# Attention scores of two units at once: float32 products of 64 contraction rows in place of split bf16 products of 128

## What is computed

```python
# x: (8, 224, 2048), context: (8, 750, 512), 32 query heads of 64, 8 key/value heads, 4 query heads to each
q = layernorm(x)                                     # split into 8 groups x 4 heads x 64
k = v = context                                      # split into 8 heads x 64
scores = einsum('bsgrd,btgd->bgrst', q, k) / 8 + mask     # mask: (224, 750)
out = einsum('bgrst,btgd->bsgrd', softmax(scores), v)
x = x + tanh(g_xattn) * out
# then layernorm(x), a routed memory of 512 slots, a small gelu network and a gate, added to x
```

## Time and profile before

| What | Value |
|---|---|
| median of 3 runs | 1175.29 us (1174.78 to 1175.48) |
| the profiled execution | 1174.98 us, its span 1173.1 us, granted clock 0.999 |
| TensorE busy | 1150.5 us (98% of the span) |
| VectorE busy | 947.2 us (81%) |
| ScalarE busy | 912.7 us (78%) |
| GpSimd busy | 889.6 us (76%) |
| chain that ended last | TensorE 76%, GpSimd 20% (its line L593 14%, L560 2%) |
| L593 (GpSimd), 448 times | 1469 ns each |
| L1312 (VectorE), 448 times | 938 ns each |
| L726 and L722 (ScalarE), 448 times each | 917 and 809 ns |
| L912, 896 times, and L923, 896 times | records of 384 and 267 ns |

### The profile page before, as it was taken

The page is one execution under the profiler, slowest core; times in us unless marked ns, Lnnn a source line. Parts: engine busy times, 40 slices in busy tenths (PEclk is TensorE's granted clock), DMA queues, the critical chain, the costliest instruction groups (busy, mean ns, idle before and its releaser), DMA issues.

```text
span 1173.1 us, 35389 instructions
## 1 busy us (share of the span) xinstructions
PE 1150.5 (98%) x14656; PEld 907.2 (77%) x14656; DVE 947.2 (81%) x2269; ACT 912.7 (78%) x1226; POOL 889.6 (76%) x804
## 2 busy tenths in 40 slices
PE   5999999999999999999999999999999999999997
PEld 3888888888888888888888888888887655655553
DVE  5888888888888888888888888888874899676775
ACT  5899898888898888898899988898881444655544
POOL 6899999999999999999999999999992110314222
PEclk9999999999999999999999999999999999999999
DMA  9421231133114212411331131122126500012224
GB/s 337 150 69 48 57 117 42 55 75 106 41 43 107 80 49 53 121 42 55 69 111 42 42 73 52 48 53 57 43 79 187 234 2 1 1 59 87 108 99 153
DMA packets 60735, 95.09 MB, mean 81 GB/s; under 512 B 35233, under 2 KB 44449, under 8 KB 56482
## 3 DMA queue, kind: packets, MB, share of 16 engines
q1 hardware_dynamic: 59858, 91.79, 25.7%
q10 hardware_dynamic: 720, 1.05, 0.3%
HBM read 71.75 MB, written 20.97 MB: 79 GB/s over the span
## 4 chain that ended last, share of the span: by engine, by line
PE 76%; POOL 20%; DMA 1%; DVE 1%; issue 1%; ACT 1%; DVEq 0%; SPq 0%; POOLq 0%
POOL arena L593 14%; PE psum L988 13%; PE psum L912 12%; PE psum L935 12%; PE psum L942 6%; PE psum L923 6%; PE psum L965 5%; PE psum L959 5%; PE psum L960 5%; PE psum L1069 3%; POOL arena L560 2%; PE psum L975 2%; PE psum L890 2%; POOL arena L613 1%; PE psum L1038 1%; POOL arena L601 1%
## 5 line engine op out<-in xcount | busy, mean ns | idle before, releaser
L593 POOL TENSOR_TENSOR arena<-arena 128x768 bf16<-128x768 f32 x448 | 651.6, 1469 | 39.7 <-ACT arena L722 37.1
L1312 DVE CUSTOM_DVE_ANT_0 arena<-psum,arena 128x750 f32<-128x750 f32 x448 | 420.3, 938 | 127.1 <-PE psum L923 121.4
L722 ACT ACTIVATE arena<-psum 128x768 f32<-128x768 f32 x448 | 362.3, 809 | 89.4 <-PE psum L942 89.3
L726 ACT ACTIVATE arena<-arena,neg_max 128x750 f32<-128x750 f32 x448 | 410.9, 917 | 3.8 <-DVE neg_max L1312 3.7
L912 PE MATMUL psum<-arena 128*128 128x512 bf16 x896 | 272.1, 384 | 0.8 <-DVE arena L1209 0.8
L935 PE MATMUL psum<-ident,arena 128*128 128x128 f32 x1792 | 268.4, 272 | 0.0
L959 PEld LDWEIGHTS psum<-arena 128*128 128x128 bf16 (+1 forms) x2688 | 194.7, 98 | 57.5
L960 PE MATMUL psum<-arena 128*128 128x64 bf16 (+1 forms) x2688 | 222.0, 193 | 0.0
L959 PE MATMUL psum<-arena 128*128 128x65 bf16 (+1 forms) x2688 | 221.7, 194 | 0.0
L960 PEld LDWEIGHTS psum<-arena 128*128 128x128 bf16 (+1 forms) x2688 | 178.5, 98 | 53.2
L935 PEld LDWEIGHTS psum<-ident,arena 128*128 128x128 f32 x1792 | 206.3, 140 | 4.3
(11 more groups left out here) (166 smaller groups left out, 1301.3 us busy)
## 6 DMA issues: line engine op xcount, KB each, us to landing
arena<-in_k_t SPq DMA_DIRECT2D x128, 187.5 KB, 3.2
arena<-in_v_rows SPq DMA_DIRECT2D x64, 192.0 KB, 2.5
out<-arena SPq DMA_DIRECT2D x12, 1024.0 KB, 3.9
arena<-in_x_top SPq DMA_DIRECT2D x8, 1024.0 KB, 5.4
arena<-in_x_rest SPq DMA_DIRECT2D x8, 768.0 KB, 4.6
spill<-arena SPq DMA_DIRECT2D x96, 64.0 KB, 2.2
arena<-spill SPq DMA_DIRECT2D x6, 1024.0 KB, 10.6
arena<-in_w_t SPq DMA_DIRECT2D x4, 1024.0 KB, 20.4
```

What stands on the lines that cost most here:

```text
L593: pool.tensor_tensor(p_lo[:, n % RING, :], p_sb[:, n % RING, :], high(p_sb[:, n % RING, :]), ALU.subtract).then_inc(p_split, 1)
L722: act.activation(p_sb[:, n % RING, :], flat_ps[:, turned_at(n):turned_at(n) + CW], ACT.Copy).then_inc(evac_a, 1)
L726: act.activation(s_sb[:, n % RING, 0:CTX], s_sb[:, n % RING, 0:CTX], ACT.Exp, bias=neg_max[:, n % 4, :], scale=-1.0).then_inc(exped, 1)
L1312: dve.tensor_tensor_reduce(s_sb[:, n % RING, 0:CTX], flat_ps[:, score_at(n):score_at(n) + CTX], mask_sb[:, max(n % UNITS - REP + 1, 0), :] ...
```

## The change

Scores of two units, a and a + 1 with a even, are computed together by `score_pair`, as float32 products straight from `q_t` and `k_raw`. `q_t` is now float32 and holds both halves of a transposed block as they come: an even unit has its 64 contraction rows in partitions 0 to 63, an odd one in 64 to 127. So each product uses one half of the array's rows. The columns of the two units are cut in three steps, so that the two halves never write one bank in the same step; a semaphore (`middle_written`) orders the two writers of the middle bank. `score_pair(k + 4)` stands at the start of every even step, ahead of the transposes, and waits until the maxima of both units of the pair before are done (`maxed >= a`).

As halves alternate with the unit's number and a window has seven units, query heads 0 and 1, and 2 and 3, change places in odd windows (`m ^ g % 2` in `add_part`), and one block of the further rows is normalised with its two heads swapped, in two instructions (`crossed`).

`split_k`, `k_lo`, `split_q` and `round_q` are gone. VectorE makes one full-height float32 copy of the query blocks per window; ScalarE makes the three first ones (`copy_first`). VectorE's maximum waits for both units of a pair, and the odd one also for the transposes of the unit three before, whose buffer it overwrites. `DVE_EVACS` is empty, so all copies of transposed exponentials stay on ScalarE.

```diff
+        SCORE_STEPS = ((slice(512, 750), slice(238, 476)), (slice(0, 274), slice(476, 750)), (slice(274, 512), slice(0, 238)))
...
-            def split_k(g):
-                pool.wait_ge(k_loaded[g % 2], 32 * (g // 2 + 1))
...
-                pool.tensor_tensor(k_lo[:, g % 2, :], k_raw[:, g % 2, :], high(k_raw[:, g % 2, :]),
-                                   ALU.subtract).then_inc(k_split, 1)
...
+                if j == 1:
+                    dst, src = crossed(xn_rest[:, j, :]), crossed(xb[:, b % 3, j, :])
+                    act.activation(dst[:, :, 1, :], src[:, :, 0, :], ACT.Identity, bias=bias, scale=scale)
+                    act.activation(dst[:, :, 0, :], src[:, :, 1, :], ACT.Identity, bias=bias, scale=scale).then_inc(rest_normed, 1)
...
+            def copy_first(i):
+                turns = FIRST_TURNS[i]
+                act.wait_ge(q_turned, i + 1)
+                act.activation(q_t[:, 0, turns[0]:turns[-1] + 1, :],
+                               mix_ps[:, FIRST_BANK[i], 0:128 * len(turns)].rearrange("p (t n) -> p t n", n=128), ACT.Copy).then_inc(q_first, 1)
...
-                    kk = high(k_raw[:, g % 2, cols]) if i == 0 else k_lo[:, g % 2, cols]
-                    pe.matmul(flat_ps[:, score_at(n) + cols.start:score_at(n) + cols.stop], q_t[:, pair % 2, half, turn, :], kk,
-                              start=(i == 0), stop=(i == 1))
...
+            def score_pair(a):
+
+                pair, at = divmod(a, 2 * UNITS)
+                for n in (a, a + 1):
+                    g = n // UNITS
+                    if n % UNITS == 0:
+                        pe.wait_ge(k_loaded[g % 2], 32 * (g // 2 + 1))
+                if pair == 0 and at in (0, REP, REP + 2):
+                    pe.wait_ge(q_first, {0: 1, REP: 2, REP + 2: 3}[at])
+                if pair >= 1 and at in (0, REP + 2):
+                    pe.wait_ge(q_copied, 2 * pair - 1 if at == 0 else 2 * pair)
+                if a >= 2:
+                    pe.wait_ge(maxed, a)
+                for i, step in enumerate(SCORE_STEPS):
+                    for half in range(2):
+                        n = a + half
+                        rows, cols = slice(D * half, D * half + D), step[half]
+                        if i == 2 and half == 1:
+                            pe.wait_ge(middle_written, a // 2 + 1)
+                        mm = pe.matmul(flat_ps[:, score_at(n) + cols.start:score_at(n) + cols.stop], q_t[rows, pair % 2, turned_slot(n), :],
+                                       k_raw[rows, n // UNITS % 2, cols], start=True, stop=True)
+                        if i == 0 and half == 0:
+                            mm.then_inc(middle_written, 1)
+                        if i == 2:
+                            mm.then_inc(scored, 1)
...
+                if k % 2 == 0 and 0 <= k + 4 < NU:
+                    score_pair(k + 4)
                 if 0 <= k + 2 < NU:
                     turn_main(k + 2)
                     turn_mid(k + 2)
-                if 0 <= k + 5 < NU:
-                    score_main(k + 5)
                 if k >= 0:
                     value(k)
...
-                if 0 <= k + 5 < NU:
-                    score_mid(k + 5)
...
-                        xs = xa[:, b, slot * GW + m * D:slot * GW + m * D + D]
+                        at = slot * GW + (m ^ g % 2) * D
+                        xs = xa[:, b, at:at + D]
...
-                    dve.wait_ge(scored, n + 1)
+                    dve.wait_ge(scored, n // 2 * 2 + 2)
+                    if n % 2 == 1 and n >= RING:
+                        dve.wait_ge(turned, n - RING + 1)
...
-                    for half in range(2):
-                        dve.tensor_copy(q_t[D * half:D * half + D, pair % 2, half, turns[0]:turns[-1] + 1, :],
...
-                if m in (4, 5) and 1 <= pair < PAIRS:
-                    split_q((window + 1) % 2, pair, m - 4, turn_range(window), 2 * (window + 3) + m - 4 + 1)
...
+                    dve.tensor_copy(q_t[:, pair % 2, turns[0]:turns[-1] + 1, :],
+                                    mix_ps[:, (window + 1) % 2, 0:128 * len(turns)].rearrange("p (t n) -> p t n", n=128)).then_inc(q_copied, 1)
```

More of the change, by code:

```diff
@@ L50 @@
 RING = 3
+DVE_EVACS = ()
 def high(ap):
@@ L61, in evac_on_dve @@
 def evac_on_dve(n):
-    return False
+    return n % (2 * UNITS) in DVE_EVACS
 def evacs_before(n, on_dve):
-    whole, part = divmod(n, UNITS)
-    return sum(whole + (1 if m < part else 0) for m in range(UNITS) if evac_on_dve(m) == on_dve)
+    whole, part = divmod(n, 2 * UNITS)
+    return sum(whole + (1 if m < part else 0) for m in range(2 * UNITS) if evac_on_dve(m) == on_dve)
 def flamingo_block(nc, x_top, x_rest, k_t, v_rows, mask, g_x, av_t, wvd_t, w1_t, wq_t, wr, wr_rows_in, keys_t, log_rel, rel, b1, w2, wvu_t,
@@ L915, in score_mid @@
-            def score_mid(n):
-                g = n // UNITS
-                half, turn = turned_slot(n)
-                if n >= 1:
-                    pe.wait_ge(maxed, n)
-                for i in range(2):
-                    cols = score_cols(n, False)
-                    kk = high(k_raw[:, g % 2, cols]) if i == 0 else k_lo[:, g % 2, cols]
-                    mm = pe.matmul(flat_ps[:, score_at(n) + cols.start:score_at(n) + cols.stop], q_t[:, g // 2 % 2, half, turn, :], kk,
-                                   start=(i == 0), stop=(i == 1))
-                mm.then_inc(scored, 1)
+            def score_pair(a):
[22 more added lines that the diff above has]
+                            mm.then_inc(scored, 1)
@@ L951, in value @@
                         pe.wait_ge(x_added, g - 1)
-                    pe.wait_ge(q_split, min(2 * g + 6, 4 * PAIRS + 2) if g else 4)
+                    if g == 0:
+                        pe.wait_ge(q_first, 2)
+                    else:
+                        pe.wait_ge(q_copied, min(g, GROUPS - 2))
                 evac_wait(pe, n)
@@ L1202, in merge_rest @@
                 ins.then_inc(rest_merged, 1)
-            def split_q(bank, pair, half, turns, count):
-                if pair == 0:
-                    dve.wait_ge(q_hi_done, count)
-                else:
-                    dve.wait_ge(q_hi_own, count - 6)
-                dve.tensor_tensor(q_t[D - D * half:2 * D - D * half, pair % 2, half, turns[0]:turns[-1] + 1, :],
-                                  mix_ps[D * half:D * half + D, bank, 0:128 * len(turns)].rearrange("p (t n) -> p t n", n=128),
-                                  q_t[D * half:D * half + D, pair % 2, half, turns[0]:turns[-1] + 1, :],
-                                  ALU.subtract).then_inc(q_split, 1)
-            def split_first(i):
-                for half in range(2):
-                    split_q(FIRST_BANK[i], 0, half, FIRST_TURNS[i], 2 * i + half + 1)
             for c in range(4):
```

84 lines of the change are left out of this document (24 added, 60 removed).

## The result

The changed kernel takes **1289.76 us** (median of 4 runs, 1289.23 to 1290.19) against 1175.08: 1.0975 times the kernel before, 95% interval 1.0956 to 1.0995, so 114.7 us more. The forecast was 1336, in a range of 1230 to 1570.

What follows compares the result with a forecast made beforehand. TensorE was taken to bound the attention, 448 units times its pitch. Scores with switches 114, copy wait 29, maxima 21, less 3 for removed work, made +161 us on the profiled execution: 1336 us, range 1230 to 1570.

Steps and rivals of the forecast that it cites:

- Passes of the scores: Score products on TensorE: halves overlap, but twelve float32 passes take seven steps in program order, 1.49 us a pair.
- Switches: TensorE going into row halves and out to float32 transposes once a pair: 0.32 us, bounds 0 and 0.5.
- Wait for the copy: Second unit's last two transposes wait for ScalarE's copy of the first: 0.13 us a pair, +29 us.
- Wait for both maxima: Next pair's scores wait for VectorE's second maximum; stalls of 0.41 (even windows) and 0.24 us (odd), +21 us.
- Taken away at nothing: GpSimd's key split and VectorE's query copies and differences, removed, were hidden by TensorE; only -3 us shows.
- A: Rival: score products of the two halves run one after the other, no overlap; about 1562 us; chance 0.20 including partial overlap.
- B: Rival: cheap switches, full overlap of the score products, no wait for the copy; about 1247 us; chance 0.15.
- C: Rival: faster, a pair of scores with its switches below 1.30 us; 1161 us; chance 0.05.
- The estimate of near 1.6 us: Score pair at a like share of 2x, after the skill's 3.07x for four row tiles; between 1.49 and A.

Runs made afterwards that it cites:

- full_height_float32: Changed kernel with the score products of both units taken over all 128 partitions, so no switch into halves; 1518.97 us, ratio 1.2925.
- both pairs of runs: Changed kernel, scores in one half against full height: 1571.91 and 1518.97 us; changed kernel plus one 4-column product, 64 against 128 rows: 1369.16 and 1315.87 us.
- additions_after: Changed kernel with all seven additions of a window behind the second maximum of a pair, not split around the first; 1274.94 us, ratio 1.0848.
- no_key_split: Kernel before with the low part of the keys made for the first two windows alone; 1174.44 us against 1175.16, ratio 0.9991.
- one_half_only: Changed kernel with the score products of both units taken from partitions 0 to 63, so none run side by side; 1571.91 us, ratio 1.3376.
- both_orders: Changed kernel with value products ahead of transposes in odd steps and all additions behind the second maximum; 1259.45 us, ratio 1.0715.

## Why the prediction was right, point by point

The direction and the three places of the loss (scores with their switches, the copy, the second maximum) were right; the sum was 161 where 114.7 were measured, mostly because one step, the order in which passes start, was wrong.

- **Passes of the scores: the step failed.** "Then the second pass of one lies beside the first pass of the next, and twelve passes take seven steps, not six" took program order for the order of starts. The first passes of both halves start together, as narrow windows show (the first window ends at 505.152, the second at 505.16, the third lies at 506.49):

```profile
505.15 0.47 PE L904 MATMUL psum<-arena 64*128 64x238 f32 x1
...
505.15 0.47 PE L904 MATMUL psum<-arena 64*128 64x238 f32 x2
...
506.32 0.36 PE L904 MATMUL psum<-arena 64*128 64x238 f32 x2
```

  The second record starts between 505.152 and 505.16. In the trace itself it is 6 or 7 ns behind the first, in each of the 224 pairs, although both passes of the first product stand ahead of it in the program. The last two passes start at 506.32, 1.17 us after the first. With their 0.20 that is 1.37 us; the sum of six steps is 1.27. The 0.1 on top is in the first pass alone; in `full_height_float32`, without any switch, the first pass is still 0.08 longer than the next. That is probably its float32 weight load, which starts with the pass and not ahead of it; no run separates this. So six steps, 1.27 and not 1.49.
- **Switches: the mechanism held, the size was near.** 0.32 us were taken. The block costs 4.17 - 2.42 - 0.13 = 1.62 us per pair; less 1.27 that leaves 0.35 for all that lies around the passes, of which 0.27 to 0.29 is the switch by both pairs of runs and the rest, by the 0.08 above, lies in the first pass. Taken together the block is +0.32 us a pair over 1.30, x 224 = 72 us, not 114. This one term holds 42 of the 46 us by which the forecast was too high. One sign named in the prediction does not work: a first transpose 0.1 us behind the last score column was to show the switch step wrong, yet a gap of about 0.1 us behind the scores was also to show it right. The gap is there (the last pass starts at 493.46 and lasts 0.20, L919 starts at 493.75); what decides is the two pairs of runs.
- **Wait for the copy: right in kind, nearly in size.** 0.13 us stand in the trace of a plain pair as forecast (1.62 + 2.42 + 0.13 = 4.17), but not in every pair. Of seven pairs, the one with four query transposes ahead of its second unit has no wait (the four take the time), and one other has 0.06 more (4.23 us). That makes 0.82 in seven pairs, x 32 = 26 us, not 29. Taking it away gave 12.8, for the reasons above.
- **Wait for both maxima: right in kind, one of two places.** The stall in even windows was put at 0.41 and is 0.48. The one in odd windows, put at 0.24, is not there: the prediction overlooked that this pair also holds the three query transposes of the odd window (0.33 us on TensorE), and D is 1.64 there, not 1.78. 15 us, not 21; `additions_after` gave them back.
- **Taken away at nothing: right.** `no_key_split` gives 0.7 us where 3 were taken, and moving copies between ScalarE and VectorE gives nothing.
- **The sum again:** 72 + 26 + 15 - 1 = 112 us, and 2 more since the two pairs with query transposes (4.51 and 4.53 us) are each 0.04 longer than their parts; measured 114.7.
- **Rivals.** A (no overlap, 1562) is what `one_half_only` shows by force, 1572; the changed kernel is not that case. Of B, the full overlap was right and the cheap switch was not, nor the missing wait for the copy. C fell: a pair of scores with its switches takes 1.62 us, over its 1.30. With the drain that the Trainium skill states (TensorEngine Tiling (Array Packing), Key Properties) the trace agrees, by 0.27 us a pair. It agrees also with the up to 2x of the Trainium skill (TensorEngine Tiling (Array Packing), Overview): twelve passes come down from 2.5 to 1.27 us here, which is all of it. The estimate of near 1.6 us from a like share of the 2x did not come out.

Two more readings. The order alone costs 96 us with the old products, but only 41 (26 + 15) with the new ones. The change takes the query differences off VectorE, which shortens D; and TensorE's own pair is 4.17 us with the new products against 3.85 with the old, which leaves more room for the same D. How the difference divides between the two was not measured. And no version with the new products or the new order beats the kernel before; the best with the new products is `both_orders`, 1259.45 us.

## What to carry to other kernels

Two row halves did halve the time of products with 64 contraction rows (2.5 to 1.27 us). Against products that already fill all rows, here by stacking high and low parts (1.30 us), that gained nothing, and each trip into halves and back cost 0.27 us, so a block must save more than that before the halves pay. When a buffer for two results is handed over as one, write down the loop: release, products, first reader, whatever that engine does in between, second reader. It sets the pace wherever it is longer than the feeding engine's own. Read what an order costs from the distance between equal starts, not from busy times or waits, in which records that outlast their columns hide a wait of 0.1 us, and a gap can be put down to an engine that had long been done.

## What the runs showed of the hardware

- Products in different row halves start within 10 ns of each other although both passes of one stand ahead of the other in the program. In `halves_apart` a pass was taken ahead of three others; that run, at 1401 us, lies between the 1290 with alternating halves and the 1572 with one half alone. How far ahead the array looks was not measured further.
- A switch into halves and out cost 0.27 us around a block of twelve passes and 0.29 us around a single product of 4 columns: about the same in both.
- Behind the block of halves the next weight load starts with its product, 0.30 us after the load before it has ended; at full height it starts 0.20 us ahead of its product, without a gap.
